# A fused two-layer kernel: weight quantisation spread evenly over the expert pairs, and the first gathers, roots and combinations of the attention stage in another order

## What is computed

```python
x = x + tanh(g_xattn[0]) * wkv_scan(layernorm(x), ctx)             # a decayed scan over the tokens
x = x + tanh(g_ffn[0])   * moe(layernorm(x))                       # 64 experts, top 4, and shared experts
x = x + tanh(g_xattn[1]) * attention(layernorm(x), ctx)            # 16 heads of 16, rms_norm of the queries
x = x + tanh(g_ffn[1])   * mlp_fp8(layernorm(x))                   # gate, up, down, block-quantised to fp8
# mlp_fp8: per 32 values  scale = max(|v|)/448, q = round_to_fp8(v/scale)*scale, of weights and activations
# rms_norm(q) = q * rsqrt(mean(q*q) + 1e-6) * w
```

## Time and profile before

| | |
|---|---|
| device time, median of 3 runs | 550.16 us (548.97 to 551.3) |
| the profiled execution: its own time | 547.86 us |
| its span in the trace, which all rows below refer to | 546.0 us |
| TensorE's granted clock, mean over the span | 0.875 of full speed |
| busy: PE, DVE, POOL, ACT | 413.0, 355.5, 239.5, 161.9 us |

### The profile page before, as it was taken

One profiled execution on the slowest core, in us unless ns is written; L12 is line 12 of the kernel. 1 busy time (PEld: TensorE's weight loads), 2 busy tenths in 40 slices (PEclk: granted clock), 3 DMA queues, 4 the chain that ended last, 5 costly groups with the idle time before them and its releaser, 6 DMA issues.

```text
span 546.0 us, 8071 instructions
## 1 busy us (share of the span) xinstructions
PE 413.0 (76%) x2711; PEld 284.1 (52%) x2711; DVE 355.5 (65%) x898; ACT 161.9 (30%) x374; POOL 239.5 (44%) x336
## 2 busy tenths in 40 slices
PE   0777653389684799999999923877887499999984
PEld 0565532234264565678888612666665145555543
DVE  3658889992644005556666825577953599999992
ACT  1444520123100245543333420334453122222220
POOL 2355443323203657765551168645310345555442
PEclk9999865589869599999999865599999599999997
DMA  7127999900055656554541522133110000000000
GB/s 205 43 76 221 281 272 219 228 14 1 1 120 164 222 166 173 161 155 102 121 120 66 170 75 83 50 91 113 60 40 1 0 1 11 10 11 10 10 10 20
DMA packets 66968, 53.19 MB, mean 97 GB/s; under 512 B 37872, under 2 KB 59504, under 8 KB 66928
## 3 DMA queue, kind: packets, MB, share of 16 engines
q1 hardware_dynamic: 56688, 34.09, 24.6%
q0 software_dynamic: 4608, 12.59, 9.2%
q10 hardware_dynamic: 5632, 6.00, 3.3%
HBM read 37.98 MB, written 14.68 MB: 96 GB/s over the span
## 4 chain that ended last, share of the span: by engine, by line
PE 41%; DVE 25%; issue 13%; POOL 12%; ACT 5%; DMA 2%; another core or an unknown queue 2%; ACTq 0%; POOLq 0%; DVEq 0%
PE psum L1098 7%; PE psum L1192 5%; PE psum L1250 5%; PE psum L1243 5%; PE psum L1274 5%; POOL arena_dn L582 3%; PE psum L1215 3%; POOL arena_up L543 3%; POOL mx_w L585 2%; DVE arena_dn L822 2%; DVE arena_up L1021 2%; PE psum L1307 2%; PE psum L1352 2%; PE psum L1271 1%
## 5 line engine op out<-in xcount | busy, mean ns | idle before, releaser
L519 POOL DMA_INDIRECT shared<-h_dram,tok_u x64 | 63.9, 999 | 61.7 <-PE psum L1215 27.9
L1383 PE MATMUL psum<-arena_dn 128*128 128x512 f32 x128 | 59.0, 615 | 3.7 <-ACT arena_dn L756 3.7
L1098 PE MATMUL psum<-ident,arena_dn 128*128 128x128 f32 x112 | 22.4, 326 | 49.5 <-DVE arena_dn L852 15.5
L997 DVE TENSOR_TENSOR h1T<-psum,h1T 128x128 f32<-128x128 f32 x32 | 9.3, 292 | 62.0 <-ACT h1T L688 49.6
L1098 PEld LDWEIGHTS psum<-ident,arena_dn 128*128 128x128 f32 x112 | 14.6, 162 | 56.3 <-issue 23.5
L1383 PEld LDWEIGHTS psum<-arena_dn 128*128 128x128 f32 x128 | 24.5, 196 | 33.7 <-issue 27.9
L1098 PE MATMUL psum<-ident,arena_up 128*128 128x128 f32 x128 | 22.0, 302 | 24.2 <-DVE arena_up L1017 10.6
L582 POOL TENSOR_TENSOR arena_dn<-arena_dn 128x512 f32<-128x512 f32 x16 | 20.3, 1270 | 44.9 <-DVE arena_dn L968 44.9
L543 POOL DMA_INDIRECT arena_up<-ys_dram,slot_u x32 | 31.3, 979 | 8.2 <-issue 8.1
L1098 PE MATMUL psum<-ident,mx_w 128*128 128x128 f32 x128 | 23.5, 320 | 12.6 <-POOL mx_w L585 9.6
L1274 PE MATMUL psum<-arena_dn,h1T 64*128 x128 | 31.9, 389 | 0.5 <-ACT h1T L699 0.5
(11 more groups left out here) (215 smaller groups left out, 981.3 us busy)
## 6 DMA issues: line engine op xcount, KB each, us to landing
ys_dram<-ysb SPq DMA_DIRECT2D x32, 256.0 KB
arena_up<-in_L_ffn_wg_dram SPq DMA_DIRECT2D x8, 512.0 KB, 8.0
arena_up<-in_L_ffn_wu_dram SPq DMA_DIRECT2D x8, 512.0 KB, 7.9
arena_dn<-in_L_ffn_wd_dram SPq DMA_DIRECT2D x4, 1024.0 KB, 11.5
va_dram<-mx_w ACTq DMA_DIRECT2D x8, 256.0 KB, 4.2
kT_dram<-mx_w ACTq DMA_DIRECT2D x8, 256.0 KB, 4.3
arena_up<-kT_dram SPq DMA_DIRECT2D x8, 256.0 KB, 2.7
arena_up<-va_dram SPq DMA_DIRECT2D x8, 256.0 KB, 3.1
```

The source lines that it names most:

```text
L519: pool.indirect_dma_start(out=xg[n % 4][:, b, :], out_offset=None, in_=h1_dram[:, :], in_offset=bass.IndirectOffsetOnAxis(ap=tok_u[:, 2 * ...
L1098: return pe.transpose(dst, src, ident[0:k, 0:k])
L1383: ins = pe.matmul(bank[2 + 2 * part + h][:, :], xTF[s][:, c, :], mx_gu[:, c, lo:lo + HW], start=(c == 0), stop=(c == C - 1))
```

## The change

Four edits, cut to their core. (1) `weight_halves`: one half a pair from pair 5 on, and then seven halves in three pairs, so that all 48 are placed with pair 31. (2) On POOL the four memsets stand ahead of the last products; only six gathers (tile 0, and half of tile 1) stand ahead of tile 0's root, and tile 1's other half and tile 0's query root behind it. (3) The gathers of a buffer count on two semaphores, one for each half, and `combine` waits half by half. (4) On DVE tile 0's queries are made one step earlier, the maxima stand ahead of the normalisation, and the copy of the queries ahead of mean and variance. On PE the transposes of tile 0's queries stand ahead of the transposes of the next tile. SP and ACT are not changed.

```diff
 def weight_halves(n):
-    return min(max(min(n, NPS - 1) - 5, 0) + 2 * max(min(n, NP - 1) - NPS + 1, 0) + 3 * max(n - NP + 1, 0), 2 * NWC)
+    return min(min(max(n - 4, 0), NPS - 5) + 7 * max(n - NPS + 1, 0) // 3, 2 * NWC)
...
-            for k in range(ahead[0], NWC):
-                weight_rescale(k)
-
             pool.wait_ge(sem("gu"), NG // 2)
             for b in range(2):
                 pool.memset(qn[b][:, :, HD:HP], 0.0).then_inc(sem("padE"), 1)
                 pool.memset(qb[b][:, D:D + 1], (D * RMS_EPS) ** 0.5).then_inc(sem("padE"), 1)
+            for k in range(ahead[0], NWC):
+                weight_rescale(k)
+
             for b in range(2):
                 pool.wait_ge(sem(f"ys_out{b}"), 16 * (NP // 2))
...
-                        .then_inc(sem(f"yk{n % 3}"), 16)
+                        .then_inc(sem(f"yk{n % 3}{k // 2}"), 16)
             gather(0, range(K))
-            gather(1, range(K))
+            gather(1, (0, 1))
+            def query_rms(n):
+                pool.wait_ge(sem("ssq"), n + 1)
+                pool.tensor_tensor(rq[n % 2], ssq[n % 2], mhalf[:, 0:1], ALU.pow).then_inc(sem("rq"), 1)
             for k in range(-1, T):
                 f = k + 1
                 if f < T:
                     inv_sqrt(rstd[:, f % 2:f % 2 + 1], mv[:, f % 2, 1:2], LN_EPS, "mvE", f + 1, "rstdE")
+                if k == -1:
+                    gather(1, (2, 3))
+                    query_rms(0)
...
                 gather(k + 3, (0, 1))
-                if k >= 0:
-                    pool.wait_ge(sem("ssq"), k + 1)
-                    pool.tensor_tensor(rq[k % 2], ssq[k % 2], mhalf[:, 0:1], ALU.pow).then_inc(sem("rq"), 1)
+                if k > 0:
+                    query_rms(k)
                 gather(k + 3, (2, 3))
...
-            def combine(n, picks):
-                for k in picks:
+            def combine(n, half):
+                dve.wait_ge(sem(f"yk{n % 3}{half}"), 32 * (n // 3 + 1))
+                for k in (2 * half, 2 * half + 1):
...
             for k in range(-2, T + 2):
                 a, b, c, e, f = k, k - 1, k - 2, k + 2, k + 1
+                if k == -1:
+                    a = 0
+                elif k == 0:
+                    a = -1
+                if 0 <= b < T:
+                    dve.wait_ge(sem("S"), b + 1)
+                    dve.tensor_reduce(qn[b % 2].rearrange("p (g j) d -> p j g d", g=4)[:, :, :, HD],
+                                      psum[:, 0:4, :].rearrange("p j (g n) -> p j g n", g=4),
+                                      AX.X, ALU.max, negate=True).then_inc(sem("smax"), 1)
                 if 0 <= f < T:
                     dve.wait_ge(sem("rstdE"), f + 1)
                     reach(dve, sem("xT_ps"), f - 1)
                     dve.tensor_scalar(xnE[f % 2], x_res[:, f, :], mv[:, f % 2, 0:1], rstd[:, f % 2:f % 2 + 1],
                                       ALU.subtract, ALU.mult).then_inc(sem("xnE"), 1)
-                if 0 <= b < T:
-                    dve.wait_ge(sem("S"), b + 1)
...
                 if 0 <= a < T:
...
+                    query_bias(a)
...
                 if e < T:
-                    dve.wait_ge(sem(f"yk{e % 3}"), 64 * (e // 3 + 1))
-                    combine(e, (0, 1))
+                    combine(e, 0)
                 if 0 <= a < T:
...
+                    query_norm(a)
                 if e < T:
-                    combine(e, (2, 3))
+                    combine(e, 1)
+                if 0 <= a < T:
+                    query_copy(a)
+                if e < T:
                     dve.bn_stats(stats[:, e % 2, :], x_res[:, e, :]).then_inc(sem("x2"), 1)
                     dve.wait_ge(sem("x2"), e + 1)
                     dve.bn_aggr(mv[:, e % 2, :], stats[:, e % 2, :]).then_inc(sem("mvE"), 1)
-                if 0 <= a < T:
-                    dve.wait_ge(sem("qT_ps"), a + 1)
-                    reach(dve, sem("S"), a - 1)
-                    dve.tensor_copy(qT[a % 2], bank[6].rearrange("p (g n) -> p g n", g=4)).then_inc(sem("qT"), 1)
...
+                if a == 0:
+                    query_turn(a)
                 if f < T:
                     pe.wait_ge(sem("xnE"), f + 1)
...
-                if 0 <= a < T:
-                    pe.wait_ge(sem("qn"), a + 1)
...
+                if 0 < a < T:
+                    query_turn(a)
```

More of the change, by code:

```diff
@@ L1018, in _ @@
                                       ALU.subtract, ALU.mult).then_inc(sem("xnE"), 1)
-                if 0 <= b < T:
-                    dve.wait_ge(sem("S"), b + 1)
-                    dve.tensor_reduce(qn[b % 2].rearrange("p (g j) d -> p j g d", g=4)[:, :, :, HD],
-                                      psum[:, 0:4, :].rearrange("p j (g n) -> p j g n", g=4),
-                                      AX.X, ALU.max, negate=True).then_inc(sem("smax"), 1)
                 if 0 <= a < T:
-                    dve.wait_ge(sem("q_ps"), a + 1)
-                    dve.tensor_tensor(qb[a % 2][:, 0:D], bank[5][:, 0:D], bias_bc[:, QB_, :], ALU.add).then_inc(sem("qb"), 1)
+                    query_bias(a)
                 if 0 <= c < T:
@@ L1295, in mx_turns, with query_turn @@
                 pe.wait_ge(sem("mxT"), 12)
+            def query_turn(a):
+                pe.wait_ge(sem("qn"), a + 1)
+                for g in range(4):
+                    ins = turn(bank[6][:, g * P:(g + 1) * P], qn[a % 2][:, 4 * g:4 * g + 4, :].rearrange("p h d -> p (h d)"))
+                ins.then_inc(sem("qT_ps"), 1)
             mx_turns()
@@ L1360, in _ @@
                     ins.then_inc(sem("o_ps"), 1)
-                if 0 <= a < T:
-                    pe.wait_ge(sem("qn"), a + 1)
-                    for g in range(4):
-                        ins = turn(bank[6][:, g * P:(g + 1) * P],
-                                   qn[a % 2][:, 4 * g:4 * g + 4, :].rearrange("p h d -> p (h d)"))
-                    ins.then_inc(sem("qT_ps"), 1)
+                if 0 < a < T:
+                    query_turn(a)
             pe.wait_ge(sem("x3"), T)
```

18 lines of the change are left out of this document (13 added, 5 removed).

## The result

| | before | after |
|---|---|---|
| median of 18 runs each, in turn on the same chip | 550.29 us | 546.46 us |
| ratio, 95% interval | | 0.9928 (0.9908 to 0.9948) |
| profiled execution: own time, span | 547.86, 546.0 us | 548.21, 546.5 us |

The change makes the kernel 0.7% faster (3.9 us; 547.1 were predicted on 550.16, a fall of 3.0). The profiled execution of the changed kernel is one of the slower of its runs, so its span shows no gain, and the stages have to be compared one by one.

A forecast was written before the change was run, and what follows sets the result against it. It took the chain of waits through POOL as the bound, the quantisation holding the gathers. Terms -2.2 -1.1 +0.4 +0.9 -1.0 = -3.0 us gave 544.9 profiled, 547.1 on the median, range 543.3 to 550.4.

The forecast's parts named there:

- step 1: Passage from experts to attention: earlier weight quantisation lets the first gather start at 314.75 instead of 316.97, -2.2 us.
- step 5: Two attention steps beside gathers: TensorE results less late, each step 10.0 us, 0.5 less than before, -1.0 us in all.
- the signs that the prediction itself named: Fails as a whole if first gather misses 314.75 by over 0.5 us; step 5 wrong if gather steps are 9 or 11.
- The other sign: Expert stage: the prediction also fails as a whole if the time between expert pairs grows.
- Step 2: Start of attention: tile 0's normalisation and query root come earlier, first scores 22.3 us after the first gather, -1.1 us.
- Step 3: Tile 0's transposed scores: tile 2's root waits for tile 3's four gathers, giving back +0.4 us.
- Step 4: Attention loop without gathers: maxima ahead of the normalisation on DVE delay the transposed scores some 0.65 us, +0.9 us in all.
- nothing is late any more: Rival, chance 0.25: both attention steps with gathers fall to 9.0 us, saving 3.0 instead of 1.0, total 545.1 us.
- `ST` beside the gathers: Slower rival, chance 0.08: transposed scores late by 2.05 us in all four steps with gathers, total 552.9 us.
- the new order eats the gain: Rival, chance 0.19: normalisation ahead of `oE` delays transposed scores in four more steps, 0.65 us each, total 549.7 us.

The follow-up runs named there:

- after_again: The changed kernel, unchanged, run again in a later group beside the kernel before: ratio 0.9911 to the kernel before.
- after_store_first: The changed kernel with the last store of expert results issued ahead of the six loads on SP's queue: ratio 0.9929 to the kernel before.
- before_quant_store: The kernel before with the new quantisation spread, POOL's memsets ahead of the last products, and the last store ahead of the six loads: ratio 0.9939.
- before_quant: The kernel before with only the new spread of the weight quantisation and POOL's memsets ahead of the last products: ratio 0.9987.
- after_gather_early: The changed kernel with POOL's first two gathers of a step ahead of its bias addition: ratio 1.0002 to the kernel before.
- before_again: The kernel before, unchanged, run again for its trace on a later group's chip: ratio 1.0001, 549.0 us.
- before_store_first: The kernel before with only the six loads moved behind the last store of expert results: ratio 1.0005.
- store_first_fill: after_store_first plus 36 more transposes of the identity in TensorE's waits of tile 0, results unread: ratio 0.983 to the kernel before, 539.62 us.

## Why the prediction was right, and where it was not

The total (-3.0, measured -3.9) is right, but that is luck: step 1 gave 1.4 us less than its term, step 5 gave 1.9 more, and the two largely cancel. By the signs that the prediction itself named, it fails as a whole, since the first gather starts at 316.97 and not within 0.5 us of 314.75, and its step 5 is wrong, since the steps with gathers are 9.0 us. The other sign, a longer time between expert pairs, did not come: from the first to the last copy of expert results it is 117.11 us before and 117.08 after. Measured values are differences of the lengths in the table, for the pair on chip A and that on chip D.

- **Step 1, the weights: -2.2; measured -0.74 and -0.88.** The quantisation ended about where the step said (308.76 against 308.1), with DVE waiting 0.63 us once for a product. What failed is the wait for the store, in two places. It was to land at 314.6, 4.9 us after its issue; by the semaphore's events it lands 5.26 us after in `before` (314.96), and 5.8 and 5.7 in `after` and `after_again`. And the gather was to start 0.15 us behind the landing; it starts 0.72 to 0.74 behind it in every trace in which the landing is what it waits for. The gain taken was two and a half to three times the measured one. By the Trainium skill (DMA: Bandwidth & Descriptors, Anatomy of one DMA), whose formula is fitted to DMAs that GpSimd issues one at a time, the store would by estimate land 2.6 us after its issue; it took 5.3 to 5.9 behind six loads. With the store first it took 2.1 us in four traces, half a microsecond less than that estimate.
- **Step 2, tile 0: -1.1; measured -1.11 and -0.95 at the first scores.** The normalisation at G+9.35 (measured 9.32), the query root at G+14.5 to 14.9 (14.22), the scores at G+22.3 (22.32): the step's working held to 0.1 us or so.
- **Step 3, +0.4.** At the third scores the balance of steps 2 and 3 should be -0.7; it is +0.10 and -1.20 (G to S2, 45.97 and 45.81 against 45.87 and 47.01). Two things come together here. In `after` the first scores' result reached DVE 1.66 us after its recorded end (341.38), beside four gathers in a row:

```profile
339.29 2.09 PE L1333 MATMUL psum<-arena_up 16*128 16x128 f32 x32
```
```profile
343.04 2.29 DVE L1043 TENSOR_REDUCE arena_up<-psum 128x16 f32<-128x2048 f32 x1 [1.79 <-remote]
```

  But that is the smaller part: the step from S0 to S1 is 12.14 us in `after`, and 11.91 in `after_store_first`, where nothing is late. On chips B and C it is 11.9 to 12.1 us with the new order of tiles 0 and 1, against 10.5 to 10.6 with the old one, so the order itself gives back 1.4 us. The trace of `after_store_first` says how: tile 2's root stands behind tile 3's four gathers, 4.67 us behind the first scores, and tile 1's query bias, query root and copy follow it; the second scores wait for that copy and no longer for the exponentials.

```profile
335.89 0.19 POOL L441 TENSOR_SCALAR small<-mv 128x1 f32<-128x1 f32 x1
```
```profile
343.13 2.09 PE L1330 MATMUL psum<-arena_up 16*128 16x128 f32 x32 [0.85 <-DVE arena_up L1030]
```

  The step priced this root only at tile 0's transposed scores (G+29.5; measured 30.2 in `after`, 29.8 in `after_again` and 29.5 in `after_store_first`), and put nothing for tile 1's queries behind it. Step 2's gain at the first scores is gone by the third ones.

- **Step 4, maxima first: +0.9; measured +0.33 and +0.33** (S4 to S7, 25.81 and 25.80 against 25.48 and 25.47). The step from S5 to S6 lost 0.31, the others nothing. The term was mis-sized, mostly by the normalisation's own length: I took its 0.81 us of the earlier trace rows along to its new place, and there it takes 0.40. The steps behind the gathers in the changed kernel:

```profile
384.37 0.40 DVE L1049 TENSOR_SCALAR arena_up<-x_res,mv,rstd 128x256 f32<-128x256 f32 x1
...
391.04 0.73 POOL L563 TENSOR_TENSOR x_res<-x_res,bias_bc 128x256 f32<-128x256 f32 x1
...
393.11 0.40 DVE L1049 TENSOR_SCALAR arena_up<-x_res,mv,rstd 128x256 f32<-128x256 f32 x1
```

In the earlier trace rows it starts with POOL's bias addition (both start on the same root); behind the maxima it runs by itself, and POOL's addition (391.04 to 391.77) is over.
- **Step 5, late results: -1.0; measured -3.06 and -2.72** (S2 to S4). The mechanism is the one that was named, the size wrong: I took the middle between 9.0 and 11.05, and the steps measure what the rival "nothing is late any more" said, to within 0.2 us a step. Its reason holds only in part. In `after` the gather (373.97) still starts before the product with the values is over (374.13), and that result is 0.4 us late; in `after_again` it starts 0.12 us behind the end and nothing is late. `ST` beside the gathers is late, as feared, but by 0.5 us and not by 2. The steps are 8.99 us here and 8.74 in `after_store_first`, where nothing is late, so this lateness costs 0.25 us a step at most.

The outcome of the rival "the new order eats the gain", though not by its mechanism, is what chips B and C would show: there the late results are absent, `before_quant_store` and `after_store_first` differ by the new orders on POOL, DVE and PE and the split semaphores, and stand at 0.9939 and 0.9929, the same within their intervals, with G-S7 0.64 us longer in the new order. The changed kernel itself was not run on such a chip. From `before_quant` (0.9987), that pair and `after_gather_early` (1.0002 on chip C, the changed kernel but for one place on POOL) I would expect it within half a per cent of the kernel before.

## What to carry to other kernels

When a wait is removed, look for what lands next, and date a DMA from a row in which somebody waits for it, not from the moment the engines fall idle; order the queue by who is waited for first, since six loads ahead of one store cost 4.5 us of E-G here (of which the times of `before_quant` and `before_quant_store` show 2.6) that the whole spreading of the quantisation couldn't buy. Two edits can each be worth little or nothing and together much (the products and the store), so undo and do them in pairs. And a gain that rests on such a timing accident as these late results should be tried on a second chip.

## What was not expected of the hardware

- **Late results come with the chip.** Each TensorE instruction's recorded end was compared with the event that its waiters see, for the semaphores whose events are all in the trace. In `before` (A) and `before_again` (D) 37 and 34 results come more than 0.3 us late (and up to 2.1), by 30 and 27 us in all, most of them in the expert stage (26 and 24), with a gather being issued before the event in every case; the changed kernel still has 35 and 30 of them. In the eight traces from B and C there is not one (at most 0.10 us), with the same instructions at the same distances. Each chip was seen in one sitting, so whether the lateness stays with a chip is not shown. The kernel before takes 9 to 11 us less on B and C. The traces place some 3 us of that in the expert stage (117.1 and 117.8 us from the first to the last copy of expert results, 114.5 to 114.7 with the same order there) and 3.5 to 4.5 between G and S7 (92.39 and 93.36 against 88.86 in `before_store_first`). That the late results are the whole of this difference is not shown: many stand where nothing waits for them.
- The Trainium skill (SBUF — State Buffer, SBUF: two separate sides) says that TensorE never waits on another engine's or a DMA's access to SBUF. The traces of B and C agree (0.07 us from the product's end to its reader's start). Those of A and D have 1.97 to 2.03 us there; whether they contradict it stays open, since no row tells whether the matrix product or only the message that it is done comes late.
- For the product with the values the lateness goes with where the gather starts: 2.03 us when it starts 0.22 us after the product does, 0.42 when it starts 0.92 us after, none when it starts behind the product's end.
- DVE's normalisation (128x256) takes 0.81 us when POOL's addition on a tile of the same shape starts with it, and 0.40 alone; when it starts 0.47 us behind the addition (345.25 against 344.78 in `after`), with 0.24 us side by side, it takes 0.41. Before the change seven of the eight ran at 0.81, after it one does. The two groups (durations in ns: least, median, most):

```profile
L1017 DVE TENSOR_SCALAR arena_up<-x_res,mv,rstd x8: 470/813/822, 327.7 to 392.9; 128x256 f32<-128x256 f32 x8
```
```profile
L1049 DVE TENSOR_SCALAR arena_up<-x_res,mv,rstd x8: 403/405/812, 326.3 to 393.1; 128x256 f32<-128x256 f32 x8
```

- A stretch of 3.9 us without work on TensorE, at the full clock, was followed by some 19 us at 1.2 GHz in `store_first_fill` (331 to 351), in which it was busy for 58% to 100% of each 2 us.
